# Four split tiles instead of two, a table of slots instead of a loop, and the softmax reciprocals on GpSimd, in a kernel of self-attention and channel-grouped normalization

## The chip, the core and the metric

The kernel runs on one core of a Trainium2 chip. The metric is the device time of one execution in microseconds. The engines of the core run side by side and each works off its own queue in order: TensorE (PE in the rows, PEld for its weight loads), VectorE (DVE), ScalarE (ACT), GpSimd (POOL) and SyncE (SP, which here only issues transfers). They wait for one another through semaphores.

## The reference, cut to what matters

x has 8 images of 128 channels and 32 x 32 = 1024 positions.

```python
x_f = einsum('oc,bcn->bon', Wf, xf) + bf          # 16 channels
x_g = einsum('oc,bcn->bon', Wg, xf) + bg          # 16 channels
x_h = einsum('oc,bcn->bon', Wh, xf) + bh          # 128 channels
s = einsum('bci,bcj->bij', x_f, x_g)              # 1024 x 1024 for each image
o = einsum('bci,bij->bcj', x_h, softmax(s, axis=-1))
y = x + gamma[0] * o
# second layer
y_n = y / max(norm(y over positions), 1e-12)
cos = einsum('bcn,bdn->cd', y_n, y_n) / B         # 128 x 128, over all images
idx = top_k(-abs(cos).T, 4)                       # each channel's partners
# mean and variance of each channel with its 3 partners, then
out = gamma * (y - mean) * rsqrt(var + eps) + beta
```

## The kernel before

An image's score matrix is cut into 8 tiles of 128 rows by 1024 columns (`t` = 0 to 7). Image 0 has a head and the last image a tail of its own. For each tile the work goes from engine to engine: TensorE computes the scores (L617) into one of two buffers `s_ps`; VectorE takes the negated row maximum `nmax` (L404); ScalarE computes the exponentials `probs` and their row sum (L318); VectorE takes the reciprocal `rinv` of the row sum (L408); and TensorE multiplies the tile with its values into `o_ps` (L636, "attend"). With two buffers the scores of a tile wait for the exponentials of the tile two before.

Attend has two forms. For a whole tile ScalarE scales the tile's values by `rinv` (L335, `vnorm`), and TensorE multiplies them in full fp32. For a split tile the values and the probabilities are each cut into a high and a low part of the rounded type fp32r, and TensorE makes three products (high x high, low x high, high x low) at that type. Tiles 3 and 7 are split (`SPLIT`): ScalarE copies the high part of `probs` (L324), and VectorE makes the high values (L415), the low part of `probs` (L418) and the low values (L421).

Beside the tiles, for each image: the projections of f and g of the next image (L606), copied by ScalarE (L308) and negated in part (L311); GpSimd adds them into `f_parts` (L266) and VectorE into `g_parts` (L427), which is how f and g are cut into high and low rows; the projection of the values (L611) with its bias (L435); the residual `y_cur` (L447), its squares (L348), its transposes (L645) and their two parts (L362, L452), the Gram matrix of the channels (L651) and its scaled sum (L460, L463, L469) with the norm made by GpSimd (L282, L289). Two copies in SBUF are made by transfers: the next image into `x_cur`, and `y_cur` into `y_all`.

The order on each engine is written out by hand in a function `stage` of each engine, which goes through the 8 tiles and runs scores 3 tiles ahead of attend (`AHEAD`) and the scaling 2 tiles ahead (`SCALED`). Images 2 to 5 run in a loop on each engine, two images to a pass; the others are written out.

Of the kernel before, what the change touches and what calls it, by code (L numbers as in the profile page):

```python
# [17 lines left out]
AHEAD = 3  # L40
SCALED = 2
SPLIT = (3, 7)
# [10 lines left out]
def build(nc, x, wide, out):  # L53
# [4 lines left out]
    assert C == P and H == 2 and T == 8 and B % 2 == 0 and B >= 4  # L58
    assert all(SCALED <= t < T for t in SPLIT)

    with ExitStack() as ctx:
# [8 lines left out]

        x_all = sb("x_all", [P, B, N])
        y_all = sb("y_all", [P, B, N])
        x_cur = sb("x_cur", [P, N])
        wd = sb("wd", [P, WIDE])
        warm = sb("warm", [P, BANK], BF16)
        fg32 = sb("fg32", [P, N])
        fg_neg = sb("fg_neg", [P, N], F32R)
        f_parts = [sb(f"f_parts{i}", [P, N], F32R) for i in range(2)]
        g_parts = [sb(f"g_parts{i}", [P, N], F32R) for i in range(2)]
        values = [sb(f"values{i}", [P, T, P]) for i in range(2)]  # L80
        probs = [sb(f"probs{i}", [P, N]) for i in range(T)]
# [4 lines left out]
        v_high = [sb(f"v_high{i}", [P, P], F32R) for i in range(len(SPLIT))]  # L86
        v_low = [sb(f"v_low{i}", [P, P], F32R) for i in range(len(SPLIT))]
# [4 lines left out]
        y_cur = sb("y_cur", [P, N])  # L92
# [8 lines left out]
        mhalf = sb("mhalf", [P, B])  # L101
        cos = sb("cos", [P, P])
# [27 lines left out]
        cur_in = sem("cur_in")  # L130
        warm_set = sem("warm_set")
        halves_set = sem("halves_set")
        zeros_set = sem("zeros_set")

        fg_proj = sem("fg_proj")
        fg_copied = sem("fg_copied")
        neg_ready = sem("neg_ready")
        g_ready = sem("g_ready")
        f_head = sem("f_head")
        f_ready = sem("f_ready")  # L140
        v_proj = sem("v_proj")
        v_ready = sem("v_ready")
        scores = sem("scores")
# [5 lines left out]
        vh_ready = sem("vh_ready")  # L149
        vl_ready = sem("vl_ready")  # L150
# [4 lines left out]
        y_kept = sem("y_kept")  # L155
# [35 lines left out]
        GROUPS = [slice(0, 1), slice(1, 3), slice(3, B)]  # L191

# [3 lines left out]
        def image(stack, b):  # L196
            return stack[:, bass.ds(b, 1), :].rearrange("p a n -> p (a n)")

        WHOLE = [t for t in range(T) if t not in SPLIT]

        def ahead(b, t, par):

            return (b, t, par) if t < T else (b + 1, t - T, 1 - par)

        def split_count(b, t):
            return len(SPLIT) * b + SPLIT.index(t) + 1
# [3 lines left out]

        def run_stages(engine, stage):

            stage(0, 0, first=True, previous=False, turn=False)
            stage(1, 1, turn=False)
            with engine.Fori(0, B // 2 - 2) as i:
                stage(2 * i + 2, 0, x_count=16 * i + 32)
                stage(2 * i + 3, 1, x_count=16 * i + 32)
            stage(B - 2, 0, load_ahead=False, x_count=8 * B)
            stage(B - 1, 1, project=False)
# [4 lines left out]
        def _(sp):  # L224
            def load(b, par):
                sp.dma_start(x_all[:, b, :], x[b]).then_inc(x_in[par], 16)

            def stage(b, par, first=False, previous=True, turn=True, project=True, load_ahead=True, x_count=16):
                if project:

                    sp.wait_ge(v_proj, H * (b + 1))
                    sp.wait_ge(x_in[1 - par], x_count)
                    sp.dma_start(x_cur[:, :], x_all[:, b + 1, :]).then_inc(cur_in, 16)
                    if load_ahead:

                        load(b + 2, par)
                if previous:

                    sp.wait_ge(y_ready, H * b)
                    sp.dma_start(y_all[:, b - 1, :], y_cur[:, :]).then_inc(y_kept, 16)  # L240
# [15 lines left out]
        def _(pool):  # L256
# [3 lines left out]
            def parts_f(b):  # L260
                for h in range(H):
                    pool.wait_ge(neg_ready, H * b + h + 1)
                    if b >= 2:

                        pool.wait_ge(scores, T * (b - 1))
# [530 lines left out]
```

## Time and profile before

| | |
|---|---|
| median of 3 runs | 214.53 us (214.19 to 214.67) |
| span of the profiled execution, first to last instruction | 211.9 us |
| time around the span (median less span) | 2.6 us |
| TensorE busy | 186.4 us, 88% of the span |
| VectorE busy | 173.7 us, 82% |
| ScalarE busy | 143.9 us, 68% |
| GpSimd busy | 34.3 us, 16% |

The profile is of one execution, whose own time is its span of 211.9 us and what lies around it. In what follows a **period** is the time from one image's step to the same step of the next image.

### The profile page before, as it was taken

The page shows a single profiled execution, that of the slowest core. Times are in us where ns is not written, and L with a number is a line of the kernel's source. Part 1 is how long each engine was busy: PE and PEld are TensorE (multiplying, and loading weights), DVE is VectorE, ACT ScalarE, POOL GpSimd, SP SyncE. Part 2 cuts the span into 40 slices and gives each one's busy share as a digit, 9 for nine tenths or more (in the row PEclk, how much of TensorE's full clock was granted, in tenths as well). Part 3 has the DMA queues.
Part 4 walks back from the last instruction along what each step waited for, and adds up shares of the span by engine and source line. Part 5 has one row for each costly group of instructions (what it writes and reads, how often), then busy time and mean ns, then how long its engine had stood idle before and what let it go on. Part 6 is the DMA issues. An engine that isn't in the chain of part 4 may idle for free.

```text
span 211.9 us, 2596 instructions
## 1 busy us (share of the span) xinstructions
PE 186.4 (88%) x727; PEld 115.2 (54%) x727; DVE 173.7 (82%) x317; ACT 143.9 (68%) x256; POOL 34.3 (16%) x39
## 2 busy tenths in 40 slices
PE   7669979999999999999999999999999999983100
PEld 3435546465765676466756675657465756462000
DVE  6588989979898889979797979887988898766660
ACT  2548976799379955995499658984799378740320
POOL 0200210034003400160007100520034001001400
PEclk9999999999999999999999999999999999997555
DMA  6240002500060007000520052002200020000198
GB/s 207 89 162 0 0 0 100 203 0 0 39 257 3 0 0 292 6 0 3 205 94 0 0 186 111 0 0 99 99 0 0 3 99 0 0 0 0 53 403 336
DMA packets 4904, 16.16 MB, mean 76 GB/s; under 512 B 544, under 2 KB 672, under 8 KB 4896
## 3 DMA queue, kind: packets, MB, share of 16 engines
q1 hardware_dynamic: 4320, 14.68, 18.4%
q10 hardware_dynamic: 576, 1.38, 1.7%
q8 instruction: 4, 0.07, 0.1%
q14 instruction: 4, 0.03, 0.0%
HBM read 4.52 MB, written 4.19 MB: 41 GB/s over the span
## 4 chain that ended last, share of the span: by engine, by line
PE 71%; DVE 13%; ACT 6%; issue 5%; POOL 1%; DVEq 0%; ACTq 0%; POOLq 0%
PE o_ps L636 40%; PE s_ps L617 11%; PE w_ps L611 6%; PE w_ps L606 6%; DVE nmax L404 3%; PE w_ps L651 3%; ACT probs L318 3%; PE w_ps L645 2%; PE o_ps L603 2%; DVE y_all L596 1%; DVE probs_low L418 1%; DVE g_parts L427 1%; DVE y_cur L447 1%; ACT probs_high L324 1%; DVE values L435 1%
## 5 line engine op out<-in xcount | busy, mean ns | idle before, releaser
L318 ACT ACTIVATE probs<-s_ps,nmax 128x1024 f32<-128x1024 f32 x64 | 70.9, 1108 | 40.5 <-DVE nmax L404 40.5
L636 PE MATMUL o_ps<-probs,vnorm 128*128 128x512 f32 x192 | 90.2, 594 | 0.5 <-DVE y_cur L447 0.5
L404 DVE TENSOR_REDUCE nmax<-s_ps 128x1 f32<-128x1024 f32 x64 | 77.9, 1218 | 10.2 <-PE s_ps L617 9.8
L617 PE MATMUL s_ps<-g_parts,f_parts 128*128 128x512 f32 x128 | 51.6, 485 | 4.6 <-ACT probs L318 2.3
L636 PEld LDWEIGHTS o_ps<-probs,vnorm 128*128 128x128 f32 x192 | 35.3, 189 | 28.8 <-issue 23.2
L266 POOL TENSOR_TENSOR f_parts<-fg,fg_neg 64x512 fp32r<-64x512 f32 x14 | 24.0, 1713 | 122.1 <-ACT fg_neg L311 122.1
L617 PEld LDWEIGHTS s_ps<-g_parts,f_parts 128*128 128x128 f32 x128 | 21.2, 190 | 20.7 <-issue 14.0
L418 DVE TENSOR_TENSOR probs_low<-probs,probs_high 128x1024 fp32r<-128x1024 f32 x16 | 19.5, 1221 | 1.3 <-ACT probs_high L324 1.2
L427 DVE TENSOR_TENSOR g_parts<-fg,fg_neg 64x512 fp32r<-64x512 f32 x16 | 13.9, 871 | 6.6 <-ACT fg_neg L311 6.5
L335 ACT ACTIVATE vnorm<-values,rinv 128x128 f32<-128x128 f32 x48 | 18.8, 391 | 0.0
L611 PEld LDWEIGHTS w_ps<-wd,x_cur 128*128 128x128 f32 x112 | 14.7, 192 | 6.7 <-issue 6.7
L324 ACT ACTIVATE probs_high<-probs 128x1024 fp32r<-128x1024 f32 x16 | 16.8, 1048 | 0.0
L606 PE MATMUL w_ps<-x_all,wd 128*128 128x512 f32 (+1 forms) x32 | 16.7, 615 | 0.0
L611 PE MATMUL w_ps<-wd,x_cur 128*128 128x128 f32 x112 | 14.8, 275 | 0.0
L308 ACT ACTIVATE fg<-w_ps,wd 128x512 f32<-128x512 f32 x16 | 10.8, 676 | 3.2 <-PE w_ps L606 3.2
L636 PE MATMUL o_ps<-probs_high,v_high 128*128 128x512 f32 x32 | 12.7, 398 | 0.1
L636 PE MATMUL o_ps<-probs_high,v_low 128*128 128x512 f32 x32 | 12.6, 394 | 0.0
L636 PE MATMUL o_ps<-probs_low,v_high 128*128 128x512 f32 x32 | 12.5, 391 | 0.0
L318 ACT ACTIVATION_READ_ACCUMULATOR probs<-s_ps,nmax 128x1 f32 x64 | 12.4, 194 | 0.0
L311 ACT ACTIVATE fg_neg<-fg,wd 128x512 fp32r<-128x512 f32 x16 | 11.6, 722 | 0.5
L447 DVE SCALAR_TENSOR_TENSOR y_cur<-o_ps,wd,x_all 128x512 f32<-128x512 f32 x14 | 10.0, 749 | 2.0 <-PE o_ps L636 1.7
L452 DVE TENSOR_TENSOR yT<-w_ps,yT 128x512 fp32r<-128x512 f32 x14 | 9.5, 682 | 2.1 <-ACT yT L362 2.1
(90 smaller groups left out, 165.7 us busy)
## 6 DMA issues: line engine op xcount, KB each, us to landing
x_all<-x_dram SPq DMA_DIRECT2D x7, 512.0 KB, 4.0
x_cur<-x_all SPq DMA_DIRECT2D x7, 512.0 KB, 3.2
y_all<-y_cur SPq DMA_DIRECT2D x7, 512.0 KB, 2.9
out_dram<-y_all SPq DMA_DIRECT2D x5, 512.0 KB, 5.8
out_dram<-y_all ACTq DMA_DIRECT2D x2, 512.0 KB, 4.1
x_all<-x_dram SPq DMA_DIRECT2D x2, 256.0 KB, 3.7
out_dram<-y_all SPq DMA_DIRECT2D x2, 256.0 KB, 2.2
wd<-wide_dram ACTq DMA_DIRECT2D x1, 256.0 KB, 4.3
```

What stands on the lines that cost most here:

```text
L266: nc.gpsimd.tensor_tensor(f_parts[b % 2][0:KP, halves[h]], fg32[0:KP, halves[h]], fg_neg[0:KP, halves[h]].bitcast(F32), ALU.add).then_inc( ...
L318: nc.scalar.activation(probs[t][:, :], s_ps[t % 2][:, :], ACT.Exp, bias=nmax[:, t:t + 1], accum_out=rsum[:, t:t + 1]).then_inc(exp_done, 1)
L324: nc.scalar.activation(probs_high[SPLIT.index(t)][:, :], probs[t][:, :], ACT.Copy).then_inc(high_ready, 1)
L335: nc.scalar.activation(vnorm[t][:, :], values[par][:, t, :], ACT.Copy, scale=rinv[:, t:t + 1]).then_inc(vn_ready, 1)
L404: nc.vector.reduce_max(nmax[:, t:t + 1], s_ps[t % 2][:, :], AX_X, negate=True).then_inc(max_ready, 1)
L418: nc.vector.tensor_tensor(probs_low[n][:, :], probs[t][:, :], probs_high[n][:, :].bitcast(F32), ALU.subtract).then_inc(low_ready, 1)
L427: nc.vector.tensor_tensor(to[0:KP, columns], fg32[rows, columns], fg_neg[rows, columns].bitcast(F32), ALU.add).then_inc(done, 1)
L447: nc.vector.scalar_tensor_tensor(y_cur[:, halves[h]], o_ps[:, halves[h]], wd[:, GAMMA:GAMMA + 1], image(x_all, b)[:, halves[h]], ALU.mult, ...
L606: return nc.tensor.matmul(w_ps[:, halves[h]], wd[:, WFG:WFG + P], image(x_all, b)[:, halves[h]], start=True, stop=True)
L611: last = nc.tensor.matmul(to[:, t * P:(t + 1) * P], source[:, t * P:(t + 1) * P], wd[:, WHT:WHT + P], start=True, stop=True)
L617: last = nc.tensor.matmul(s_ps[t % 2][:, h], f_parts[par][:, t * P:(t + 1) * P], g_parts[par][:, h], start=True, stop=True)
L636: last = nc.tensor.matmul(o_ps[:, halves[h]], weights[:, :], rows[:, halves[h]], start=(t == 0 and n == 0), stop=(t == T - 1 and n == len( ...
```

## The change

- Tiles 2, 3, 6 and 7 are split. For 3 and 6 (`VECTOR_SPLIT`) ScalarE makes the high part of the scaled probabilities (L355) and VectorE the low part in one instruction with two SBUF inputs (L430). For 2 and 7 (`POOL_SPLIT`) GpSimd does all three steps: it scales `probs` in place (L273), copies the high part (L279) and subtracts for the low part (L284). The values are no longer scaled for a split tile; GpSimd cuts them in two parts, once for each half image (L260, L262).
- All reciprocals of the row sums, 8 an image, are made by GpSimd as a power of -1 (L268), in its queue between the split steps. VectorE makes none.
- The projections of f and g are no longer copied. ScalarE negates them from PSUM (L339) and VectorE adds from PSUM over all 128 rows (L438); the g rows are brought to partition 0 by a transfer of 128 KB for each half (`g_low`). GpSimd no longer makes `f_parts`.
- The residual is written in place over `x_all`. The transfers into `x_cur` and `y_all` are gone.
- There is no loop. Every engine goes through the slots -4 to 63 (one a tile), and tables say in which slot of an image each step stands. Scores run 4 tiles ahead of attend. ScalarE scales one slot behind its exponential, and the low part stands 2 slots behind on VectorE and 1 slot behind on GpSimd.

```diff
-AHEAD = 3
-SCALED = 2
-SPLIT = (3, 7)
+AHEAD = 4
+LAGS = (0, 0, 1)
+SCALE_LAG = 1
+LOW_LAG = 2
+VECTOR_SPLIT = (3, 6)
+POOL_SPLIT = (2, 7)
+SPLIT = (2, 3, 6, 7)
+PE_FG, ACT_NEG, DVE_PARTS = (0, 1), (0, 0), (1, 1)
+PE_V, DVE_V, POOL_V = (4, 5), (5, 5), (5, 6)
+PE_T, ACT_T, DVE_T = (2, 3), (1, 3), (3, 4)
+ACT_SQUARE, POOL_NORM = 4, 4
+PE_GRAM, DVE_GRAM, PE_TURN, DVE_ADD = 6, 6, 7, 8
...
+            for b in range(1, B):
+                for h in range(H):
+                    sp.wait_ge(parts_ready, H * b + h + 1)
+                    if b >= 2:
+                        sp.wait_ge(scores, T * (b - 1))
+                    sp.dma_start(g_low[b % 2][0:KP, halves[h]].bitcast(F32),
+                                 fg_parts[b % 2][KP:P, halves[h]].bitcast(F32)).then_inc(g_in[h], 16)
...
+            def invert_sum(b, t):
+                pool.wait_ge(exp_done, T * b + t + 1)
+                nc.gpsimd.tensor_tensor(rinv[:, t:t + 1], rsum[:, t:t + 1], minus_one[:, 0:1],
+                                        ALU.pow).then_inc(rinv_ready, 1)
+            def scale_probs(b, t):
+                pool.wait_ge(rinv_ready, T * b + t + 1)
+                nc.gpsimd.tensor_scalar(probs[t][:, :], probs[t][:, :], rinv[:, t:t + 1], 1.0,
+                                        ALU.mult, ALU.mult).then_inc(pool_scaled, 1)
+            def high_probs(b, t):
+                n, count = SPLIT.index(t), pool_split_count(b, t)
+                pool.wait_ge(pool_scaled, count)
+                nc.gpsimd.tensor_copy(probs_high[n][:, :], probs[t][:, :]).then_inc(pool_high, 1)
+            def low_probs(b, t):
+                n, count = SPLIT.index(t), pool_split_count(b, t)
+                pool.wait_ge(pool_high, count)
+                nc.gpsimd.tensor_tensor(probs_low[n][:, :], probs[t][:, :], probs_high[n][:, :].bitcast(F32),
+                                        ALU.subtract).then_inc(pool_low, 1)
...
+            def low_part(b, t):
+                n = SPLIT.index(t)
+                dve.wait_ge(high_ready, vector_split_count(b, t))
+                nc.vector.scalar_tensor_tensor(probs_low[n][:, :], probs[t][:, :], rinv[:, t:t + 1],
+                                               probs_high[n][:, :].bitcast(F32), ALU.mult,
+                                               ALU.subtract).then_inc(low_ready, 1)
```

On GpSimd's queue, before: the first parts of f and then the work of one image.

```order
L272 TENSOR_TENSOR f_parts<-fg,fg_neg 64x512
L266 TENSOR_TENSOR f_parts<-fg,fg_neg 64x512 x4
L282 TENSOR_SCALAR nsq<-stats 128x1
L289 TENSOR_TENSOR rnorm<-nsq,mhalf 128x1
L266 TENSOR_TENSOR f_parts<-fg,fg_neg 64x512 x2
```

On the same queue, after: from the last of a group of four reciprocals (tiles 4, 5, 6 and 7) over tile 7, the reciprocals of the next image's tiles 0, 1 and 2, and the first steps of tile 2.

```order
L268 TENSOR_TENSOR rinv<-rsum,minus_one 128x1 x4
L273 TENSOR_SCALAR probs<-probs,rinv 128x1024
L279 CAST probs_high<-probs 128x1024
L268 TENSOR_TENSOR rinv<-rsum,minus_one 128x1
L284 TENSOR_TENSOR probs_low<-probs,probs_high 128x1024
L290 TENSOR_SCALAR nsq<-stats 128x1
L297 TENSOR_TENSOR rnorm<-nsq,mhalf 128x1
L268 TENSOR_TENSOR rinv<-rsum,minus_one 128x1
L260 CAST v_high<-values 128x256
L262 TENSOR_TENSOR v_low<-values,v_high 128x256
L268 TENSOR_TENSOR rinv<-rsum,minus_one 128x1
L273 TENSOR_SCALAR probs<-probs,rinv 128x1024
```

GpSimd had four instructions an image. It now has eight reciprocals, six steps on 128x1024 and six smaller ones, and the reciprocals of tiles 0 to 3 stand behind split steps.

On VectorE's queue, before: the second half of an image, tiles ahead 4 to 7.

```order
L427 TENSOR_TENSOR g_parts<-fg,fg_neg 64x512
L404 TENSOR_REDUCE nmax<-s_ps 128x1
L408 RECIPROCAL rinv<-rsum 128x1
L452 TENSOR_TENSOR yT<-w_ps,yT 128x4x128
L404 TENSOR_REDUCE nmax<-s_ps 128x1
L408 RECIPROCAL rinv<-rsum 128x1
L452 TENSOR_TENSOR yT<-w_ps,yT 128x4x128
```

On the same queue, after: slots 1 to 4 of an image, which take the maxima of tiles 5, 6, 7 and of the next image's tile 0; the first low part is tile 3's, the second tile 6's.

```order
L425 TENSOR_REDUCE nmax<-s_ps 128x1
L430 SCALAR_TENSOR_TENSOR probs_low<-probs,rinv,probs_high 128x1024
L438 SCALAR_TENSOR_TENSOR fg_parts<-w_ps,wd,fg_neg 128x512 x2
L425 TENSOR_REDUCE nmax<-s_ps 128x1 x2
L468 TENSOR_TENSOR yT<-w_ps,yT 128x4x128
L425 TENSOR_REDUCE nmax<-s_ps 128x1
L430 SCALAR_TENSOR_TENSOR probs_low<-probs,rinv,probs_high 128x1024
L468 TENSOR_TENSOR yT<-w_ps,yT 128x4x128
```

The reciprocals are gone from VectorE, both halves of the f and g parts stand together, and they and the maxima of tiles 6 and 7 stand behind the low part of tile 3.

## Rows read from the trace of the kernel before

**Rows 1.** The page's first part: busy us, share of the span, instructions.
```profile
PE 186.4 (88%) x727; PEld 115.2 (54%) x727; DVE 173.7 (82%) x317; ACT 143.9 (68%) x256; POOL 34.3 (16%) x39
```
**Rows 2.** One period: length, then busy us of PE, PEld, DVE, ACT, POOL.
```profile
72.49:94.82 22.33, 22.33 (x90) 14.07 (x90) 19.43 (x36) 17.30 (x32) 4.32 (x4) 1.00 0.19 71
```
**Rows 3.** The chain that ended last: start, us, what (scores, a whole tile, a split tile).
```profile
75.57 0.46 PE s_ps L617 x2
76.03 1.72 PE o_ps L636 x4
...
79.10 1.38 PE o_ps L636 x6
```
**Rows 4.** Groups by line and shape: count, busy us, mean ns, idle before.
```profile
L418 DVE TENSOR_TENSOR probs_low<-probs,probs_high 128x1024 fp32r<-128x1024 f32 x16 | 19.5, 1221 | 1.3 <-ACT probs_high L324 1.2
...
L324 ACT ACTIVATE probs_high<-probs 128x1024 fp32r<-128x1024 f32 x16 | 16.8, 1048 | 0.0
```
**Rows 5.** Timeline, GpSimd and below it VectorE: start, us, instruction.
```profile
23.19 1.29 POOL L266 TENSOR_TENSOR f_parts<-fg,fg_neg 64x512 fp32r<-64x512 f32 x1 [12.65 <-ACT fg_neg L311]
26.27 1.25 POOL L266 TENSOR_TENSOR f_parts<-fg,fg_neg 64x512 fp32r<-64x512 f32 x1 [1.79 <-ACT fg_neg L311]
...
45.03 1.80 POOL L266 TENSOR_TENSOR f_parts<-fg,fg_neg 64x512 fp32r<-64x512 f32 x1 [17.50 <-ACT fg_neg L311]
...
49.50 0.21 POOL L282 TENSOR_SCALAR nsq<-stats 128x1 f32<-128x1 f32 x1
49.80 0.57 POOL L289 TENSOR_TENSOR rnorm<-nsq,mhalf 128x1 f32<-128x1 f32 x1
...
23.43 1.59 DVE L427 TENSOR_TENSOR g_parts<-fg,fg_neg 64x512 fp32r<-64x512 f32 x1
...
44.99 0.69 DVE L427 TENSOR_TENSOR g_parts<-fg,fg_neg 64x512 fp32r<-64x512 f32 x1 [0.77 <-ACT fg_neg L311]
```
**Rows 6.** Timeline, VectorE and below it ScalarE: how closely instructions follow.
```profile
33.13 1.22 DVE L404 TENSOR_REDUCE nmax<-s_ps 128x1 f32<-128x1024 f32 x1
...
36.45 0.75 DVE L447 SCALAR_TENSOR_TENSOR y_cur<-o_ps,wd,x_all 128x512 f32<-128x512 f32 x1
...
37.13 0.75 DVE L447 SCALAR_TENSOR_TENSOR y_cur<-o_ps,wd,x_all 128x512 f32<-128x512 f32 x1
...
30.35 0.39 ACT L335 ACTIVATE vnorm<-values,rinv 128x128 f32<-128x128 f32 x1
30.64 1.04 ACT L324 ACTIVATE probs_high<-probs 128x1024 fp32r<-128x1024 f32 x1
...
34.38 1.12 ACT L318 ACTIVATE probs<-s_ps,nmax 128x1024 f32<-128x1024 f32 x1 [1.60 <-DVE nmax L404]
35.39 0.19 ACT L318 ACTIVATION_READ_ACCUMULATOR probs<-s_ps,nmax 128x1 f32 x1
35.48 0.39 ACT L335 ACTIVATE vnorm<-values,rinv 128x128 f32<-128x128 f32 x1
```
**Rows 7.** Transfers: KB each, median us from issue to landing.
```profile
x_cur<-x_all SPq DMA_DIRECT2D x7, 512.0 KB, 3.2
...
out_dram<-y_all SPq DMA_DIRECT2D x2, 256.0 KB, 2.2
```
**Rows 8.** Timeline: the head, attend of tile 2 (images 1 and 7), last residual.
```profile
9.36 1.73 DVE L427 TENSOR_TENSOR g_parts<-fg,fg_neg 64x512 fp32r<-64x512 f32 x1
11.12 1.29 DVE L435 TENSOR_TENSOR values<-o_ps,wd 128x512 f32<-128x512 f32 x2
...
17.87 0.19 ACT L318 ACTIVATION_READ_ACCUMULATOR probs<-s_ps,nmax 128x1 f32 x1
...
42.64 1.88 PE L636 MATMUL o_ps<-probs,vnorm 128*128 128x512 f32 x4
...
175.42 1.88 PE L636 MATMUL o_ps<-probs,vnorm 128*128 128x512 f32 x4
...
186.72 0.75 DVE L525 SCALAR_TENSOR_TENSOR y_all<-o_ps,wd,x_all 128x512 f32<-128x512 f32 x1 [1.05 <-PE o_ps L636]
```

More of the change, by code:

```diff
@@ L57, in build @@
     KP = 4 * 16
[L58 to L59 removed]
+    assert C == P and H == 2 and T == 8 and B >= 4 and H == len(PE_FG)
     with ExitStack() as ctx:
@@ L191, in build, with split_values_of, tile_at, before @@
         GROUPS = [slice(0, 1), slice(1, 3), slice(3, B)]
+        WHOLE = [t for t in range(T) if t not in SPLIT]
+        def split_values_of(h):
+            its = [t for t in SPLIT if t // TH == h]
+            step = its[1] - its[0] if len(its) > 1 and len({b - a for a, b in zip(its, its[1:])}) == 1 else 1
+            return slice(its[0], its[-1] + 1, step)
+        SPLIT_VALUES = [split_values_of(h) for h in range(H)]
         def shifts_for(b):
             return next(n for n, g in enumerate(GROUPS) if b < g.stop) + 1
[L196 to L206, printed above, removed]
+        def tile_at(slot):
+            return divmod(slot, T) if 0 <= slot < T * B else None
+        def before(b, t, slot):
+            i = b - 1 - slot // T
+            return i if slot % T == t and 0 <= i < L else None
+        def vector_split_count(b, t):
+            return len(VECTOR_SPLIT) * b + VECTOR_SPLIT.index(t) + 1
+        def pool_split_count(b, t):
+            return len(POOL_SPLIT) * b + POOL_SPLIT.index(t) + 1
         def whole_count(b, t):
             return len(WHOLE) * b + WHOLE.index(t) + 1
[L211 to L219, printed above, removed]
         block = ctx.enter_context(nc.Block())
@@ L280, in _, with norm @@
+            def norm(b):
                 if b < L:
@@ L290, in _ @@
                                         ALU.pow).then_inc(rnorm_ready, 1)
+            for slot in range(-AHEAD, T * B):
+                b, t = divmod(slot, T)
+                its = tile_at(slot + AHEAD)
+                if its is not None:
+                    invert_sum(*its)
+                for lag, part in enumerate((scale_probs, high_probs, low_probs)):
+                    its = tile_at(slot + AHEAD - LAGS[lag])
+                    if its is not None and its[1] in POOL_SPLIT:
+                        part(*its)
+                for h in range(H):
+                    if slot == -1 and b < 0:
+                        split_values(0, h)
+                    if b >= 0 and b < L and t == POOL_V[h]:
+                        split_values(b + 1, h)
+                i = before(b, t, POOL_NORM)
+                if i is not None:
+                    norm(i)
+            norm(L)
             pool.wait_ge(table_in, 1)
@@ L640, in attend, with transposes @@
                         last.then_inc(first_half, 1)
                 last.then_inc(probs_used, 1)
-            def transposes(source, to, tiles, first=0):
-                for t in tiles:
-                    last = nc.tensor.transpose(to[:, (t - first) * P:(t - first + 1) * P],
-                                               source[:, t * P:(t + 1) * P], ident)
-                return last
+            def transposes(b, h, to):
+                pe.wait_ge(y_ready, H * b + h + 1)
+                if b + 2 < B:
+                    pe.wait_ge(parts_ready, H * (b + 2) + h + 1)
+                if b == L - 1 and h == 0:
+                    pe.wait_ge(gram_scaled, L - 1)
+                if b == L - 1 and h == 1:
+                    pe.wait_ge(gram_added, L)
+                for n in range(TH):
+                    t = h * TH + n
+                    last = nc.tensor.transpose(to[:, n * P:(n + 1) * P], x_all[:, b, t * P:(t + 1) * P], ident)
+                last.then_inc(yT_made, 1)
```

537 lines of the change are left out of this document (251 added, 286 removed).

## The prediction

> **What bounds the kernel now.** First the page's busy shares [rows 1]: TensorE 88%, VectorE 82%, GpSimd 16%. A share over the whole span is only a hint, so next comes one period by itself [rows 2]: of 22.33 us TensorE is busy 22.33, VectorE 19.43, ScalarE 17.30, GpSimd 4.32. Last, the chain that ended last [rows 3]: in the middle images it is TensorE alone, scores 0.46, a whole tile 1.72, a split tile 1.38. So TensorE sets the period, VectorE has some 3 us of slack in it, and GpSimd is nearly free. From attend of tile 2 in image 1 to the same in image 7 it is 175.42 - 42.64 = 132.8 us [rows 8], 22.13 a period.
>
> **TensorE.** Two more tiles are split: 2 x (1.72 - 1.38) = 0.68 off a period. All else on TensorE stays in kind and count, so if TensorE still sets the period it is 22.33 - 0.68 = 21.65 us. No added instruction stands on TensorE; the question is whether the others deliver in time.
>
> **VectorE and ScalarE** lose work in sum (eight reciprocals, the scaled values, the copies of f and g), and neither sum comes near the period. What matters on them is order. After the maximum of tile 5, VectorE waits for the high part of tile 3, makes its low part (L430), then both f and g parts, then the maxima of tiles 6 and 7. ScalarE needs those maxima for exponentials 6 and 7, and GpSimd's long run begins at the exponential of tile 7.
>
> **GpSimd, what one instruction costs.** The trace has two kinds. Two inputs, 64x512, where it came first: 1.25 to 1.29. A power on one column: 0.57, with 0.09 between an instruction and one that waits for it [rows 5]. A one-column TENSOR_SCALAR takes 0.21 [rows 5], which I take as the fixed part. Then two inputs over 512 are 0.21 + 1.04, over 1024 they are 2.3, over 256 they are 0.73. No row shows one input over 1024 (L273 and L279). From below: ScalarE's copy of that shape, 1.05 [rows 4]. From above: as much as two inputs over 1024, 2.3. Nearest are two inputs over 512, which read as many elements: 1.25. I take 1.15, between 1.05 and 1.25, and keep 1.05 to 1.7 for the range. One input over 256 is taken as 0.21 + 0.26 = 0.47, so a cut of the values (L260, L262) is 0.47 + 0.09 + 0.73 = 1.29.
>
> The Trainium skill (GPSIMD Engine Reference, Engine selection) says that on this engine one-input work runs at roughly line rate and two-input work about twice as slow as on VectorE. By its 1.2 GHz, an estimate, L273 and L279 would be near 1.06 us each and the sum below about 3 us lower. No run so far shows a one-input operation of this size.
>
> **Two engines meet at the SBUF.** GpSimd's addition at 23.19 lasts to 24.48. VectorE's addition with two SBUF inputs starts at 23.43 and lasts 1.59 instead of 0.69: it ends 0.54 after GpSimd's, as if it had stood until then with 0.15 of its start-up done. At 44.99 VectorE comes first, and GpSimd's addition takes 1.80 instead of 1.25 [rows 5]. So the later of the two waits for the earlier. Now VectorE's operations with two large SBUF inputs are its two low parts an image (L430, 1.22 like L418 [rows 4]). All its others read PSUM.
>
> The Trainium skill states this as an exclusive lock held for the whole instruction, and counts in a VectorE instruction with two SBUF inputs against a GpSimd one that reads SBUF (SBUF — State Buffer, Who interferes with whom). By that rule the change puts GpSimd's work where it costs VectorE most. The trace agrees for the additions above; for L430 and for the one-input forms no row shows it.
>
> Before, GpSimd worked 4 us a period, so meetings were few. Now the low part of tile 3 meets it always: ScalarE can make its high part only after GpSimd's reciprocal of tile 3, and right behind that reciprocal GpSimd starts the low part of tile 2, 2.3 us, while the high part takes 1.05. VectorE stands until it ends. And the low part of tile 6 falls into GpSimd's unbroken run and puts 1.22 - 0.15 = 1.07 into it.
>
> **The ring.** Start at the end of GpSimd's low part of tile 2, which is what attend of tile 2 waits for. VectorE: low part of tile 3, 1.07 more. Two parts of f and g (PSUM and SBUF in, 128x512, as L447) at 0.68 [rows 6], 1.36. Maximum of tile 6 to its exponential 1.25 (33.13 to 34.38), exponential to the next instruction 1.10, scaling of tile 5 0.29 (30.35 to 30.64), exponential of tile 7 to the end of its sum 1.20 and 0.04 to the next engine [rows 6]. Together 6.31 us. The maximum of tile 7 lies under this.
> Then GpSimd without a pause: five reciprocals (7, 0, 1, 2, 3) 2.85; two low parts 4.6; the norm 0.21 + 0.09 + 0.57 = 0.87; two cuts of the values 2.58; four waits 0.36; the meeting with tile 6's low part 1.07: 12.33 us. Four one-input steps at 1.15: 4.60. Together 16.93.
> The ring is 6.31 + 16.93 = 23.24 us, over TensorE's 21.65 and over the 22.13 of before. Its other inputs come earlier: the exponentials of tiles 0 to 3 are due when TensorE gets to their scores, 3 us or more ahead of their reciprocals. Six periods cost 6 x (23.24 - 22.13) = +6.7 us.
>
> **The transfer of g** (128 KB, new) starts when both parts are made, 1.07 + 1.36 = 2.4 us after the ring's start, and takes 2.2 to 3.2 us [rows 7]; I take 2.2, the smaller transfer's. The next image's first scores wait for it until 4.7 to 5.7. They also wait for the exponential of tile 6, 1.07 + 1.36 + 1.25 + 1.24 = 4.9. From there TensorE has about 17.5 us to attend of tile 2, so it is there at 22.4 to 23.2: hidden by the ring, but barely.
>
> **Head.** The first maximum moves ahead of the two value additions (1.29), and the g part beside it no longer meets GpSimd (1.73 becomes 0.69) [rows 8]: 2.3 us earlier. The exponential of tile 2 ended at 18.06 and now ends at 15.75. GpSimd then makes reciprocal, scale, high part, reciprocal of tile 3, low part: 0.57 + 0.09 + 1.15 + 0.09 + 1.15 + 0.57 + 2.3 = 5.9, to 21.7. From there the ring once, without the norm and one wait with it: 21.7 + 23.24 - 0.9 = 44.0, against 42.64: +1.4 us. The zeros move from VectorE to an idle GpSimd; nothing.
>
> **Tail.** From attend of tile 2 in the last image: 6.31 less the parts of f and g, 4.95; then reciprocal 0.57, two waits 0.18, two steps 2.3, the meeting 1.07, low part 2.3, a wait 0.09; then half an attend 0.69: 12.15, against 186.72 - 175.42 = 11.3 [rows 8]: +0.8. The Gram product now stands ahead of the last attend and no longer before the last transposes; they then wait for the residual, and I take 0.5 off. The rest of the tail is the same.
>
> **Sum** against the profiled execution: 211.9 + 6.7 + 1.4 + 0.8 - 0.5 = 220.3; with the 2.6 us around the span, 222.9 us. That is 8.4 over the median.
>
> **Rivals.**
> One, no meeting of these forms (a gain): L430 and GpSimd's steps don't hold each other up. Then the ring loses about 1.07 at each of its two places and is 21.1, TensorE sets 21.65, six periods bring -2.9, head +0.3, tail -0.9: 211.0 us. For it: only additions with two SBUF inputs on both sides were seen. Against it: L430 has two such inputs, and every GpSimd step reads SBUF.
> Two, dear one-input steps: 1.7 us each and up puts 4 x 0.55 = 2.2 into each ring, seven rings and half a one in the tail: 239 us; at 2.3 us each, 256. The only ground is that no row shows them.
> Three, the ring is broken somewhere (GpSimd gets ahead in the middle of an image, or its steps run at 1.0 or less): the period is between 21.65 and 22.4, where TensorE or the transfer of g limits, and the time 212 to 216.
> Four, the lock also lets the reciprocal of tile 4 in ahead of VectorE's low part at the ring's start: +0.57 a period, 227 us. This lies inside the forecast.
>
> **How the numbers follow.** The forecast, ring at 1.05 to 1.4 us a step and with or without rival four, 218 to 231: 0.60. Rival one, 0.15. Rival two above 232: 0.12. Rival three, 0.10; 0.03 are left. About 0.2% is what a measurement of this kernel can tell from no change, so faster has rival one and half of three, 0.19; same 0.04; slower 0.77. The range from 211 to 232 leaves out rival two and a little below.
>
> **What would show it.** In the profile of the changed kernel: TensorE idle before attend of tile 2 with GpSimd's low part as the releaser; VectorE's L430 well above 1.22 us in the mean, or its wait; a GpSimd busy share near 80%; a period of 23.2 us. L273 and L279 at 1.05 to 1.25 us. Wrong would be: L430 at 1.22 everywhere (rival one); one-input steps at 1.7 or more (two); a chain of TensorE alone in the middle images (one or three).

## The result: 219.56 us, 2.3% slower

| | before | after |
|---|---|---|
| median | 214.53 us | 219.56 us (219.25 to 219.95, 4 runs) |
| ratio | | 1.023, 95% interval 1.022 to 1.025 |
| span of the profiled execution | 211.9 us | 217.3 us |

The forecast was 222.9 us, slower. The sign and the mechanism came out; the size was 3.3 us too large. The page of the kernel after answers to [rows 1]: busy us, share of the span, instructions; then the TensorE clock in 40 slices, and the chain that ended last, by engine.

```profile
PE 188.5 (87%) x759; PEld 121.7 (56%) x759; DVE 165.6 (76%) x219; ACT 135.8 (62%) x231; POOL 148.9 (69%) x171
...
PEclk9976999999999999999999999999999999999555
...
POOL 47%; DVE 15%; issue 15%; ACT 10%; PE 9%; DVEq 0%; ACTq 0%; POOLq 0%
```

TensorE is still busiest, but the chain is GpSimd's now. One period, in the columns of [rows 2], is 22.34 us:

```profile
67.73:90.07 22.34, 22.21 (x94) 14.76 (x94) 19.30 (x24) 16.35 (x29) 18.02 (x21) 1.00 0.13 35
```

TensorE's busy time would pass for a full engine, though its own period is 21.55 us (below). What it loses lies in small gaps: attend of tile 4 starts 5.24 us behind attend of tile 2 (95.31, 90.07), and 4.58 in a kernel that TensorE bounds (e6). So the bound is read from the chain. Here is one turn of it, from the reciprocal of tile 3 to the reciprocal of tile 7 and on: start, us, what.

```profile
87.09 0.52 POOL rinv L268
...
87.63 1.16 ACT probs_high L355
...
88.81 0.04 DVE probs_low L430
88.85 0.64 issue
89.49 0.02 DVEq L437
89.51 1.42 issue
90.93 1.40 DVE fg_parts L438 x2
92.33 1.14 DVE nmax L425
...
93.49 0.02 ACT probs L346
...
96.09 0.07 issue
96.16 0.56 POOL rinv L268
96.72 0.09 issue
96.81 1.13 POOL probs L273
97.94 0.06 issue
97.99 1.90 POOL probs_high L279
99.89 0.52 POOL rinv L268
100.41 2.37 POOL probs_low L284
```

No TensorE stands in it. The 2.1 us of issue from 88.85 on are VectorE in its low part: what holds it there is no semaphore, so the chain has no name for it. Behind the last row GpSimd goes on without a gap up to the next low part of tile 2 (109.89 to 112.26). This is the ring of the prediction, link by link.

Where the 5.4 us of the span came from, with attend of tile 2 at 45.39 in image 1 and at 179.42 in the last [rows 8 for before]:

| stretch | before | after | difference | predicted |
|---|---|---|---|---|
| start to attend of tile 2, image 1 | 42.64 | 45.39 | +2.75 | +1.4 |
| six periods | 132.78 | 134.03 | +1.25 | +6.7 |
| from there to the last residual | 11.30 | 13.18 | +1.88 | +0.8 |
| the rest | 25.18 | 24.70 | -0.48 | -0.5 |

The errors of the rows stand against each other: the periods came out 5.4 us under the forecast, head and tail 2.4 over it, and it is partly luck that the total is nearer than its terms. The remaining 0.3 us is around the span, 2.3 us where 2.6 was taken.

The row of the six periods hides where its 1.25 us are. Before, the first five from image 1 on took 111.42 us (22.21 to 22.33 each), and the last one, with no f and g behind it, 21.36, from this row to the 175.42 of [rows 8]:

```profile
154.06 1.88 PE L636 MATMUL o_ps<-probs,vnorm 128*128 128x512 f32 x4
```

After, all six took 22.33 or 22.34. So a middle period hardly changed (22.28 to 22.34 in the mean): GpSimd's ring took back what the split saved on TensorE. 0.97 of the 1.25 us is the last period, in which TensorE has less to do but the ring does not.

The groups by line and shape: count, busy us, mean ns, idle before. They answer to [rows 4].

```profile
L268 POOL TENSOR_TENSOR rinv<-rsum,minus_one 128x1 f32<-128x1 f32 x64 | 42.0, 657 | 40.3 <-ACT probs L346 40.2
L284 POOL TENSOR_TENSOR probs_low<-probs,probs_high 128x1024 fp32r<-128x1024 f32 x16 | 38.1, 2379 | 0.1
L430 DVE SCALAR_TENSOR_TENSOR probs_low<-probs,rinv,probs_high 128x1024 fp32r<-128x1024 f32 x16 | 31.6, 1978 | 8.5 <-ACT probs_high L355 8.5
...
L279 POOL CAST probs_high<-probs 128x1024 fp32r<-128x1024 f32 x16 | 23.5, 1468 | 1.1
...
L273 POOL TENSOR_SCALAR probs<-probs,rinv 128x1024 f32<-128x1024 f32 x16 | 17.9, 1120 | 1.6
```

L273, the one-input step that nothing met, took 1.12 us. L279 has two prices that its mean hides, and L430 is far above the 1.22 us that the low part took before and the 1.28 us that it takes where it starts ahead of GpSimd (e11). The timeline shows both places, GpSimd first and VectorE below it: start, us, instruction, in brackets the idle time before.

```profile
87.56 2.36 POOL L284 TENSOR_TENSOR probs_low<-probs,probs_high 128x1024 fp32r<-128x1024 f32 x1
89.89 1.53 POOL L268 TENSOR_TENSOR rinv<-rsum,minus_one 128x1 f32<-128x1 f32 x1
...
97.99 1.90 POOL L279 CAST probs_high<-probs 128x1024 fp32r<-128x1024 f32 x1
...
107.22 1.04 POOL L279 CAST probs_high<-probs 128x1024 fp32r<-128x1024 f32 x1
...
88.81 2.20 DVE L430 SCALAR_TENSOR_TENSOR probs_low<-probs,rinv,probs_high 128x1024 fp32r<-128x1024 f32 x1 [0.49 <-ACT probs_high L355]
90.93 1.40 DVE L438 SCALAR_TENSOR_TENSOR fg_parts<-w_ps,wd,fg_neg 128x512 fp32r<-128x512 f32 x2
...
97.15 1.84 DVE L430 SCALAR_TENSOR_TENSOR probs_low<-probs,rinv,probs_high 128x1024 fp32r<-128x1024 f32 x1 [0.41 <-ACT probs_high L355]
```

At 88.81 VectorE's low part of tile 3 comes while GpSimd's of tile 2 runs (to 89.92), and ends at 91.01, 1.09 us behind it. GpSimd's next instruction, the reciprocal of tile 4, then takes 1.53 instead of 0.55: VectorE, which was already waiting, went first. At 97.15 the scaling of tile 7 (96.81 to 97.93) is in the way of tile 6's low part, and then that one is in the way of L279, which takes 1.90 instead of 1.04.

### The profile page after: what moved, and what is told of

It reads as the page before. It is cut to its first block, busy times and chain, and to the rows that moved or that the text cites. A ratio compares the mean times of both kernels' runs of the same rounds, so it can differ in the third digit from the quotient of the medians.

```text
span 217.3 us, 2462 instructions
## 1 busy us (share of the span) xinstructions
PE 188.5 (87%) x759; PEld 121.7 (56%) x759; DVE 165.6 (76%) x219; ACT 135.8 (62%) x231; POOL 148.9 (69%) x171
## 4 chain that ended last, share of the span: by engine, by line
POOL 47%; DVE 15%; issue 15%; ACT 10%; PE 9%; DVEq 0%; ACTq 0%; POOLq 0%
POOL probs_high L279 10%; POOL probs_low L284 10%; POOL rinv L268 9%; POOL probs L273 8%; DVE nmax L425 5%; POOL v_low L262 5%; DVE fg_parts L438 5%; ACT probs L346 4%; ACT probs_high L355 3%; PE o_ps L664 2%; POOL v_high L260 2%; POOL rnorm L297 2%; PE w_ps L616 2%; PE s_ps L643 2%; PE o_ps L600 2%
## 5 line engine op out<-in xcount | busy, mean ns | idle before, releaser
L268 POOL TENSOR_TENSOR rinv<-rsum,minus_one 128x1 f32<-128x1 f32 x64 | 42.0, 657 | 40.3 <-ACT probs L346 40.2
L664 PE MATMUL o_ps<-probs,vnorm 128*128 128x512 f32 x128 | 60.3, 595 | 0.3 <-DVE x_all L461 0.3
L643 PE MATMUL s_ps<-g_low,fg_parts 128*128 128x512 f32 x128 | 51.1, 482 | 4.3 <-ACT probs L346 3.4
L284 POOL TENSOR_TENSOR probs_low<-probs,probs_high 128x1024 fp32r<-128x1024 f32 x16 | 38.1, 2379 | 0.1
L430 DVE SCALAR_TENSOR_TENSOR probs_low<-probs,rinv,probs_high 128x1024 fp32r<-128x1024 f32 x16 | 31.6, 1978 | 8.5 <-ACT probs_high L355 8.5
L643 PEld LDWEIGHTS s_ps<-g_low,fg_parts 128*128 128x128 f32 x128 | 21.3, 195 | 17.1 <-ACT probs L346 7.7
L279 POOL CAST probs_high<-probs 128x1024 fp32r<-128x1024 f32 x16 | 23.5, 1468 | 1.1
L355 ACT ACTIVATE probs_high<-probs,rinv 128x1024 fp32r<-128x1024 f32 x16 | 18.3, 1144 | 2.8 <-POOL rinv L268 2.8
L273 POOL TENSOR_SCALAR probs<-probs,rinv 128x1024 f32<-128x1024 f32 x16 | 17.9, 1120 | 1.6
L616 PE MATMUL w_ps<-x_all,wd 128*128 128x512 f32 x32 | 17.9, 652 | 0.0
L339 ACT ACTIVATE fg_neg<-w_ps,bias_neg,wd 128x512 fp32r<-128x512 f32 x16 | 12.3, 769 | 7.3 <-PE w_ps L616 7.2
```

The costliest lines, as they stand in the source:

```text
L268: nc.gpsimd.tensor_tensor(rinv[:, t:t + 1], rsum[:, t:t + 1], minus_one[:, 0:1], ALU.pow).then_inc(rinv_ready, 1)
L273: nc.gpsimd.tensor_scalar(probs[t][:, :], probs[t][:, :], rinv[:, t:t + 1], 1.0, ALU.mult, ALU.mult).then_inc(pool_scaled, 1)
L279: nc.gpsimd.tensor_copy(probs_high[n][:, :], probs[t][:, :]).then_inc(pool_high, 1)
L284: nc.gpsimd.tensor_tensor(probs_low[n][:, :], probs[t][:, :], probs_high[n][:, :].bitcast(F32), ALU.subtract).then_inc(pool_low, 1)
L355: nc.scalar.activation(probs_high[SPLIT.index(t)][:, :], probs[t][:, :], ACT.Copy, scale=rinv[:, t:t + 1]).then_inc(high_ready, 1)
L430: nc.vector.scalar_tensor_tensor(probs_low[n][:, :], probs[t][:, :], rinv[:, t:t + 1], probs_high[n][:, :].bitcast(F32), ALU.mult, ALU.sub ...
```

## The experiments

Each is the kernel after with the edit shown. "Attend" is attend of tile 2, in image 0, in image 1 and so on; periods are between images from 1 on, the last one apart, which has no f and g behind it. All times are medians.

**Do the meetings make the ring the bound?** VectorE's low part reads one tensor from SBUF instead of two; the kernel leaves out the subtraction of the high part.

```diff
-                nc.vector.scalar_tensor_tensor(probs_low[n][:, :], probs[t][:, :], rinv[:, t:t + 1],
-                                               probs_high[n][:, :].bitcast(F32), ALU.mult,
-                                               ALU.subtract).then_inc(low_ready, 1)
+                nc.vector.tensor_scalar(probs_low[n][:, :], probs[t][:, :], rinv[:, t:t + 1], None,
+                                        ALU.mult, ALU.add, accum_out=junk[:, 0:1]).then_inc(low_ready, 1)
```

> VectorE's two low parts an image read one SBUF tensor instead of two (the high part is not subtracted, so their low part is wrong; everything else is as in the changed kernel). The theory is a ring of GpSimd's run and VectorE's reply, in which the two meetings at the SBUF cost 0.97 us (VectorE behind the low part of tile 2: 2.20 to 1.22) and 0.86 us (GpSimd's high part of tile 7 behind VectorE: 1.90 to 1.04). Expected by it: both durations fall to 1.2 to 1.3 and 1.04, the ring falls from 22.34 to about 20.5, TensorE takes over at about 21.65, so six periods bring -4.1, and about -1.8 from the last image's run: 213 to 214.5 us. Rival, GpSimd's load or TensorE's own waits set the period and the meetings only fill idle time: 219 us and a period of 22.3.

212.85 us (212.41 to 214.29), 0.993 of before (0.991 to 0.995); period 21.55. The chain and the two groups that had met:

```profile
PE 77%; DVE 8%; ACT 4%; POOL 4%; issue 3%; DVEq 0%; ACTq 0%; POOLq 0%
...
L431 DVE TENSOR_SCALAR_CACHE_REDUCE probs_low<-probs,rinv 128x1024 fp32r<-128x1024 f32 x16 | 20.5, 1279 | 4.1 <-ACT probs_high L356 4.1
...
L280 POOL CAST probs_high<-probs 128x1024 fp32r<-128x1024 f32 x16 | 16.6, 1040 | 1.1
```

The copy is back at the 1.04 us that it takes when nothing holds it up, the low part at the 1.28 that is its own length in e11, the chain is TensorE's, and 6.7 us are gone. With this form, which has one SBUF input, the meetings are gone, and with them the bound. The edit changes the instruction along with its inputs; no run changes the inputs alone.

**How long is the ring without them?** TensorE hides it in that run. So the same edit, and four more powers of one column in GpSimd's run, which bring the ring out again.

```diff
+                    if its[1] == 1:
+                        for n in range(4):
+                            nc.gpsimd.tensor_tensor(spare[:, n:n + 1], minus_one[:, 0:1], minus_one[:, 0:1], ALU.pow)
```

> VectorE's low parts with one SBUF input as in the first experiment (their low part is wrong), and four more powers on one column behind the reciprocal of tile 1 to keep the ring above TensorE. Ring theory with both meetings priced from the trace of the changed kernel: 22.34 - 0.97 - 0.86 + 4 x 0.52 = 22.59 a period. If only the meeting behind the low part of tile 2 were in the ring: 23.45; if only that of tile 7: 23.56; if neither: 24.42. The time would be 220.5 to 221.5 us for the first.

223.18 us (222.34 to 224.27), over what was expected. Periods are 22.66 to 22.71, one is 23.26. The four powers took 2.08 us in the chain, so the ring without meetings is 22.68 - 2.08 = 20.60 us, and the two meetings cost it 22.34 - 20.60 = 1.74 us. The rows of the kernel after say the same: 2.20 - 1.28 at L430 and 1.90 - 1.04 at L279 are 1.78. The time was missed at the ends (attend in image 1 stood at 46.65, 1.3 us later than in the kernel after) and by the odd period, in which the transfer of g stood in the chain. Its row in the chain, and the scores that waited for it in TensorE's timeline:

```profile
93.43 3.87 DMA g_low<-fg_parts
...
97.44 0.70 PE L647 MATMUL s_ps<-g_low,fg_parts 128*128 128x512 f32 x2 [1.02 <-DMA g_low<-fg_parts]
```

The usual time of this transfer is 2.2 us. The load of the next image was issued right behind it, at 93.94, but it stands as close behind the others (117.19 behind 116.68, say), and those took 2.2. What delayed this one is open.

**Is it GpSimd's run that counts, instruction by instruction?** One power more, once in the run (behind the reciprocal of tile 1) and once outside (behind that of tile 5).

```diff
+                    if its[1] == 1:      # e3; 5 in e4
+                        nc.gpsimd.tensor_tensor(spare[:, 0:1], minus_one[:, 0:1], minus_one[:, 0:1], ALU.pow)
```

> One more power on one column, on a spare tile, right behind the reciprocal of tile 1 on GpSimd, that is inside its unbroken run. Ring theory: 0.52 us more in each of some seven turns: period 22.86 and 219.6 + 3.6 = 223.2 us. Rival, the run has slack: within 0.5 us of 219.6.

> The same instruction behind the reciprocal of tile 5 instead, where GpSimd waits 2.6 us for the next exponential. The load on GpSimd is that of the run with the instruction inside. Ring theory: nothing in the middle images, 219.3 to 219.9 us, at most +0.5 if the last image's run is touched. Rival, GpSimd's total load sets the time: as much slower as with the instruction inside, 223 us.

Inside: 223.7 us (223.07 to 224.18), 0.5 over what was expected; period 22.87, so +0.53 a period for an instruction of 0.52 in the chain. Outside: 220.27 us (219.26 to 220.34), also over the expected range; period 22.33, nothing. The 0.7 us that it has over the kernel after stands wholly before attend in image 1 (46.25 against 45.39), where the clock of its head was lower than after's, 0.68 of full speed even from 21 to 23 us; its one run with a higher mean clock (0.941, the others 0.934) took 219.26. So an instruction behind tile 1's reciprocal, inside the run, cost its full length in each of the six periods, and one behind tile 5's reciprocal none. That every place from the reciprocal of tile 7 to the low part of tile 2 counts alike is argued from the chain.

**What do the reciprocals themselves cost there?** VectorE makes all eight.

```diff
-                                        ALU.pow).then_inc(rinv_ready, 1)
...
+                nc.vector.reciprocal(rinv[:, t:t + 1], rsum[:, t:t + 1]).then_inc(rinv_ready, 1)
```

> The eight reciprocals of an image go back to VectorE (its reciprocal instruction, one slot behind the maximum), nothing else changes. Ring theory: five of them stand in GpSimd's run, 5 x 0.52 = 2.6 us, so the ring falls to about 19.8 and TensorE sets 21.65: -4.1 over six periods, -1 in the head (two of them stood ahead of the first low part), -0.5 to -1 in the tail: 213 to 214.5 us. Rival, the period comes from the new order of the slots or from the transfer of g and not from GpSimd: stays at 218 to 219.6 us. Rival, a reciprocal in VectorE's queue holds back its maxima: slower than 219.6.

215.74 us (215.43 to 216.31), over the expected range; period 21.83, chain 75% TensorE. Five reciprocals of 0.52 leave the ring, and 3.8 us the time. But VectorE's low part (L426 here) still meets (its mean is 1.94), and the period stays 0.28 over the 21.55 of the run with one input. The chain shows TensorE alone, since the matmul's own row has no idle time; the weight load beside it has, ahead of the first scores of the next image. TensorE's weight load, and below it VectorE's low part of tile 3:

```profile
92.79 0.30 PEld L642 LDWEIGHTS s_ps<-g_low,fg_parts 128*128 128x128 f32 x2 [0.25 <-ACT probs L338]
...
86.94 2.11 DVE L426 SCALAR_TENSOR_TENSOR probs_low<-probs,rinv,probs_high 128x1024 fp32r<-128x1024 f32 x1
```

These scores wait for the exponential of tile 6. Its maximum stands behind the f and g parts, and those behind the low part that GpSimd held up. The wait is there in every period, 0.24 to 0.27 us from image 3 on, and puts the second matmul of these scores 0.62 us behind the matmul ahead of them instead of 0.34. The run with both edits (below), whose low part takes 1.39 us in the mean, has 0.34 and a period of 21.55. So the meeting still costs 0.28 us a period by another way, from VectorE over ScalarE to TensorE.

**Is another instruction out of the run worth the same?** The second cut of the values goes from ahead of the reciprocal of tile 3 to behind the low part of tile 2.

```diff
-PE_V, DVE_V, POOL_V = (4, 5), (5, 5), (5, 6)
+PE_V, DVE_V, POOL_V = (4, 5), (5, 5), (5, 7)
```

> The second cut of the values stands one slot later in GpSimd's queue, behind the low part of tile 2 instead of ahead of the reciprocal of tile 3. No instruction is added or taken away. Ring theory: 1.15 us leave the run (0.40 + 0.09 + 0.74 less the overlap), the ring falls to 21.2 and TensorE sets 21.7 to 21.8: 6 x 0.6 = 3.5 us less, and with no help to the head or the last image 215.6 to 216.2 us. Rival one, GpSimd's total load sets the period: no change from 219.6. Rival two, the moved cut now wins the SBUF ahead of VectorE's low part of tile 3: 0.4 us back a period, ring 21.6, hardly to be told from the first.

213.98 us (213.73 to 214.69, 10 runs), 0.998 of before (0.996 to 0.999); period 21.54. That is 1.6 us under what was expected (six periods of 0.6 less, and no help elsewhere): one number in a table gives back the whole loss. 5.3 us of span went: 4.0 in five periods, 0.6 in the head, 0.7 in the last image and its tail. The meeting at the ring's start changed too, in VectorE's timeline below GpSimd's:

```profile
84.11 2.36 POOL L284 TENSOR_TENSOR probs_low<-probs,probs_high 128x1024 fp32r<-128x1024 f32 x1
86.42 1.39 POOL L260 CAST v_high<-values 128x256 fp32r<-128x256 f32 x1
...
86.26 1.30 DVE L430 SCALAR_TENSOR_TENSOR probs_low<-probs,rinv,probs_high 128x1024 fp32r<-128x1024 f32 x1
```

VectorE again goes ahead of GpSimd's next instruction, and now it is the cut (1.39 us instead of 0.40) that waits, outside the ring.

**Do the two add up?** Both edits.

> Two edits of the changed kernel: the second cut of the values one slot later, and the reciprocals made by VectorE. Theory (each alone already brings the ring to TensorE's period or near it; together they bring no more in the middle images, 21.55 us): between 212.5 and 213.8 us, the difference from 213.98 us of the cut alone being in the head and the tail. Rival (the gains of the two add up, because the ring still limits with either alone): 211.5 us or less.

213.41 us (213.17 to 214.17), 0.996 of before (0.994 to 0.998); period 21.55. They don't: either brings the ring to TensorE's period or near it, and from there nothing is left to gain in the middle images.

**The head.** The projections of f and g for image 1 stand between the scores of tiles 1 and 2, where TensorE was idle.

```diff
-                    if 0 <= b < L and t == PE_FG[h] == 0:
+                    if 0 < b < L and t == PE_FG[h] == 0:
                         project_fg(b + 1, h)
+                    if slot == 1 - AHEAD:
+                        project_fg(1, h)
...
-                    if 0 <= b < L and t == PE_FG[h] > 0:
+                    if 0 < b < L and t == PE_FG[h] > 0:
```

> The projections of f and g of image 1 stand between the scores of tiles 1 and 2 of image 0, where they stood before the change, instead of in slots 0 and 1. Theory: in the head TensorE had 2.08 us with nothing to do from 11.0 us, and the granted clock then stood at 0.5 (1.2 GHz) from about 13 to 20 us, where the kernel before stayed at 1.0 all through its first 28 us; the projections fill the gap. Expected: 1.0 throughout the head, exponential of tile 2 some 0.4 us earlier, attend of tile 2 of image 0 at 23.5 to 24.0 instead of 24.98, in all 0.5 to 1.5 us less: 218.0 to 219.0 us. Rival, the clock falls for another reason: it stays at 0.5 there and the time moves by less than 0.3 us. The period stays at 22.34 either way.

218.12 us (217.84 to 220.67), ratio 1.020 (1.013 to 1.027). Attend in image 1 is at 44.27 instead of 45.39; the period stays 22.33. The time is in the expected range, but not for the expected reason: the clock did not hold, it fell later, to 0.50 from 17 to 19 us.

**The tail.** The squares and the norm of the last image alone are made earlier.

```diff
-                i = before(b, t, POOL_NORM)
+                i = before(b, t, POOL_NORM if b < L else 1)
...
-                i = before(b, t, ACT_SQUARE)
+                i = before(b, t, ACT_SQUARE if b < L else 0)
```

> The changed kernel with the squares and the norm of the last image alone made early in its tail (ScalarE's squares in slot 0 instead of 4, GpSimd's norm in slot 1 instead of 4), so that the norm no longer stands behind GpSimd's split steps of tile 7. Theory (the tail's excess is VectorE's Gram step, which waits for the norm and has the residual of tile 7 behind it): from attend of tile 2 to the last residual 13.2 becomes 12.4 to 12.6 us, 218.7 to 219.0 us in all. Rival (the excess is GpSimd's run of tile 7 itself, and attend of tile 7 sets the residual): 13.1 to 13.2 us as before, 219.4 to 219.7 us. The period stays at 22.34 by both.

219.27 us (219.09 to 219.97), which can't be told from the kernel after. The stretch itself can be: from attend of tile 2 (179.77) to the last residual (192.34) it took 12.57 us instead of 13.18. In its profiled run the head was 0.35 us later than in that of the kernel after. VectorE's rows, of the kernel after first:

```profile
191.95 0.35 DVE L475 TENSOR_SCALAR gram_high<-w_ps,rnorm 128x128 f32<-128x128 f32 x1 [3.83 <-POOL rnorm L297]
...
192.60 0.74 DVE L461 SCALAR_TENSOR_TENSOR x_all<-o_ps,wd,x_all 128x512 f32<-128x512 f32 x1
```

and with the edit:

```profile
190.61 0.35 DVE L475 TENSOR_SCALAR gram_high<-w_ps,rnorm 128x128 f32<-128x128 f32 x1 [2.16 <-PE w_ps L686]
192.34 0.75 DVE L461 SCALAR_TENSOR_TENSOR x_all<-o_ps,wd,x_all 128x512 f32<-128x512 f32 x1 [0.99 <-PE o_ps L664]
```

The Gram step no longer waits for the norm, and the residual waits for its attend, as it did before the change.

**All together.** The late cut, the early projections, the early norm of the tail, and the first cut of the values ahead in the head; once with the reciprocals on VectorE (e8), once on GpSimd (e10). New beside the edits shown:

```diff
+                if slot == -3:
+                    split_values(0, 0)
+                if slot == -2:
+                    split_values(0, 1)
...
-                    if slot == -1 and b < 0:
-                        split_values(0, h)
```

> The reciprocals on VectorE, the second cut one slot later, the projections of image 1 in the gap of the head, the cuts of image 0 while GpSimd still waits for tile 2, and in the last image the squares in slot 0 and the norm in slot 1, so that VectorE's gram step and the last residual don't wait behind GpSimd's low part of tile 7. Ring theory: TensorE sets every period, 21.65 to 21.7 (six of them -4.1), head -1.5 to -2.3, tail -1.5 to -2.0: 211.3 to 212.5 us, under the kernel before by 1 to 1.5%. Rival, the four-tile split has no gain left to give once GpSimd is out of the way: 214.5 or more.

> Four edits together: the second cut of the values one slot later, the first projections of f and g early in the head, the first cut of the values early, and the squares and the norm of the last image early. The reciprocals stay on GpSimd. Theory (once the ring is shorter than TensorE's own 21.6 us, the place of the reciprocals is indifferent): the period is 21.55 us, and the time that of the same four edits with the reciprocals on VectorE, 211.2 us, plus what four reciprocals put into the head and the tail, 0.5 to 1.0: 211.7 to 212.3 us. Rival (GpSimd's reciprocals hold back the scores although the period doesn't show it): 213 us and up.

e8: 211.19 us (211.17 to 211.37), 0.1 us under what was expected, 0.984 of before (0.983 to 0.986), faster than both kernels. e10: 212.39 us (211.74 to 212.63), 0.991 (0.989 to 0.993), 0.1 us over what was expected. Both have a period of 21.55: in the middle images it is indifferent who makes the reciprocals, once the ring is under TensorE's time.

## Why the prediction was right, and where its sizes were off

**The bound moved as said.** TensorE's own period was put at 21.65 us; five kernels whose ring is hidden show about 21.55. The ring is over it, and what had been put down as its links are its links: no step of the order was wrong.

**Rival one, no meeting of these forms,** is out: the first low part at 2.20 us and the fall of the low part to 1.28 and of L279 to 1.04 when the second input goes. The Trainium skill (SBUF — State Buffer, Who interferes with whom) says that an instruction of VectorE with two SBUF inputs contends with one of GpSimd that reads SBUF. The trace agrees, also for the copy of one input (1.90 instead of 1.04) and for a power on one column (1.53 instead of 0.55), and the form with one SBUF input didn't meet (1.28). **Rival two** is out: the one-input steps took 1.12 and 1.04 us. **Rival four** is out: the reciprocal of tile 4 came behind VectorE's low part. **Rival three** gave a period up to 22.4, and 22.34 lies within it, but not by its mechanism: the ring was whole, only shorter.

Some of the prediction's sums don't fit their own terms. Rival three at a period of 22.4 is 217.8 us by the forecast's other terms, not at most 216. A one-input step of 1.4 us together with rival four makes 234 us, not 231. Rival one's 211.0 leaves out the 0.5 of the tail and doesn't show its head and tail terms; the run without meetings (e1) took 212.85, with the six periods 4.35 us shorter than before (2.9 in the sum) and the head 2.6 longer (0.3). The 22.13 that the ring was held against is the mean with the short last period; the total is right with it, but against a middle period of before, 22.28, a ring of 22.34 is next to nothing.

**The mis-sized term is GpSimd's run:** 16.93 us in the sum, 16.1 in the trace (96.16 to 112.26). Its parts, from the chain:

| | in the sum | measured |
|---|---|---|
| four one-input steps | 4.60 | 4.33 |
| two cuts of the values | 2.58 | 2.33 |
| five reciprocals | 2.85 | 2.64 |
| meeting with tile 6's low part | 1.07 | 0.86 |
| two low parts | 4.60 | 4.74 |
| norm and waits | 1.23 | 1.25 |

With the reply of VectorE and ScalarE at 6.24 instead of 6.31 the ring is 0.9 us shorter than the 23.24 forecast. That is 4% of the ring, but what a period costs is the ring less the 22.13 of before: 1.1 was forecast and 0.2 came, times six. The one value that was chosen was 1.15 us for a one-input step, where the row of ScalarE's copy gave 1.05 as the lower bound. Part of two others comes from one source: an instruction in a row of them takes the length of its row less some 0.03 us, since the next starts under its end; L268 has 0.55 in the timeline and 0.52 in the chain. The rest of the cuts is the copy over 256, 0.40 us where 0.47 was taken.

The Trainium skill (GPSIMD Engine Reference, Engine selection) says that GpSimd runs one-input work at roughly line rate. The trace agrees: the steps took 1.04 and 1.12 us, and the prediction's estimate of 1.06 us from that page was nearer than the value taken.

**Head: +1.4 forecast, +2.75 measured.** The step that failed is that TensorE's work was taken at the speed of before. The granted clock in the kernel after (us, PE, PEld, DVE, ACT, POOL, clock), and TensorE's row in which it fell:

```profile
13.00:15.00 2.00, 1.92 (x4) 0.94 (x4) 1.24 (x2) 1.44 (x4) 1.13 (x2) 0.54 0.00 0
15.00:17.00 2.00, 0.64 (x2) 0.21 (x2) 2.00 (x3) 1.47 (x3) 0.19 (x1) 0.50 0.00 0
17.00:19.00 2.00, 2.00 (x4) 1.28 (x5) 1.31 (x3) 1.23 (x3) 1.83 (x3) 0.50 0.00 0
19.00:21.00 2.00, 2.00 (x4) 0.72 (x3) 0.27 (x1) 1.70 (x3) 2.00 (x3) 0.75 0.00 0
...
13.08 2.35 PE L643 MATMUL s_ps<-g_low,fg_parts 128*128 128x512 f32 x4 [2.08 <-ACT probs L346]
```

0.50 is 1.2 GHz, where before had 1.00 (2.4 GHz) all through its head. TensorE had worked 1.2 us and then stood 2.08 us for the exponential of tile 0, because the projections of f and g, which had stood in that place, now stand behind the scores of tile 4. The scores of tile 2 (the first two matmuls at 13.08) took 1.17 instead of 0.46 us, and the exponential of tile 2 ended at 16.73 instead of the 15.75 forecast. The first turn then didn't start at GpSimd's low part but at the second projection, to which TensorE came late. The chain there:

```profile
18.01 1.71 PE w_ps L616 x2
19.71 1.92 PE o_ps L664 x4
21.64 0.47 PE s_ps L643 x2
22.11 1.72 PE o_ps L664 x4
23.83 0.87 PE w_ps L616 x2
24.70 0.02 issue
24.72 0.79 ACT fg_neg L339
```

The low part of tile 2 then ended at 22.56 instead of 21.7. The maximum behind the parts began at 26.29, 3.73 us after it, where the ring in the middle has 2.41. These are 0.9 and 1.3 us late; 0.8 less in GpSimd's run leaves 1.4. Moving the projection took 1.1 us out. How much of the head is the clock alone isn't separated: e8 and e10 have 0.50 and 1.00 from 15 to 21 us and reach attend in image 0 at 23.36 and 22.48, but attend in image 1 at 43.67 and 43.62. Nor is it shown why the clock fell. The kernel before had as long a gap on TensorE (2.27 us, up to 11.19) and kept 1.00; with the gap of 2.08 us filled the clock still fell, only later (e5); and TensorE's busy time in e8 and e10 is the same up to 15 us (2.00, 1.5 and 0.73 us in the stretches of 2 us from 9 on).

**Tail: +0.8 forecast, +1.88 measured.** The run up to the last attend was right, 11.61 us (179.42 to 191.03) against 11.46. The failed step is "then half an attend 0.69": the residual came 1.57 behind. 0.61 of it is the norm, which had been made where GpSimd idled and now stood behind the low part of tile 7, with VectorE's Gram step before the residual (e9); 0.97 is the half attend with its waits. The prediction had moved the Gram product, and not asked what its input was queued behind.

**The transfer of g** took 2.2 us and was hidden, as forecast; "but barely" was right as well: in the middle images its second half landed 0.1 to 0.2 us before the scores that need it began (94.61 and 94.75), and in e7, where it once took 3.87 us, it came out.

## What to carry to other kernels

- When work moves to an idle engine, add up the engine's run between its input and the output that others wait for, and then the reply of the others: it is this ring against the period that decides. Here GpSimd at 69% busy set the period with TensorE at 87%, and one instruction of 0.5 us was worth 0.5 us inside the run and nothing outside it. A ring that just reaches the old period eats the whole gain and leaves no other mark on the period.
- A forecast as a difference of two near numbers (23.24 against 22.13) has the error of the whole ring, and the number of before should be a middle period where the ring is one. Price the terms by how far apart instructions start, not by the length of their rows, and give the range for the difference.
- In the head and the tail, ask of each wait what its input is queued behind, and whether TensorE gets a gap that it didn't have.

## What the runs showed of the hardware

- A VectorE instruction with two SBUF inputs that waits for a GpSimd instruction goes ahead of GpSimd's next one: seen in L268 (1.53 instead of 0.55) and in L260 (1.39 instead of 0.40). The one that was held up ends a little less than its own length after the other: L430, 1.28 us long where it comes first (e11), ends 1.09 us after.
- GpSimd's one-input instructions on 128x1024 took 1.04 us (copy to fp32r) and 1.12 us (product with a column), the two-input one 2.38.
- One kernel's times follow the mean clock of the run: the kernel after took 219.25 and 219.31 us at 0.946 and 0.947, and 219.81 and 219.95 at 0.934. An effect of half a microsecond has to be read from the stretch, not from the median.
